# x1 of three supertiles in four turned by VectorE from blocks in device memory, and another order in the first two bodies

## What is computed

```python
xn = layer_norm(x) * gamma + beta
Q, K, V, gate = xn @ WQ.T + bQ, xn @ WK.T + bK, xn @ WV.T + bV, silu(xn @ Wg.T + bg)
for t: h = alpha * h + k_t v_t^T;  o_t = q_t h          # 16 heads, state 64 x 64
x1 = norm(x + x + (o * gate) @ WO.T + bO)               # no scale, no shift
gf = global_net(mean over the sequence of x1)           # 3 small layers
out = x1
for _ in range(3):                                      # coupling_net: 4 layers, GELU
    coupling = 0.1 + range * (0.7 * gf + 0.3 * coupling_net(out) - 0.5) * 2
    out = out + coupling * twist(out)
result = norm(x1 + out)
```

## Time and profile before

| | |
|---|---|
| median of 3 runs | 1736.63 us (1735.86 to 1736.78) |
| profiled execution, its own time | 1735.65 us |
| its span, first to last instruction | 1733.8 us |
| TensorE busy | 1670.2 us, 96% of the span |
| VectorE, ScalarE, POOL busy | 65%, 43%, 29% |
| mean granted TensorE clock | 0.990 |

### The profile page before, as it was taken

The page is one execution under the profiler, slowest core; times in us unless marked ns, Lnnn a source line. Parts: engine busy times, 40 slices in busy tenths (PEclk is TensorE's granted clock), DMA queues, the critical chain, the costliest instruction groups (busy, mean ns, idle before and its releaser), DMA issues.

```text
span 1733.8 us, 49923 instructions
## 1 busy us (share of the span) xinstructions
PE 1670.2 (96%) x21648; PEld 1329.6 (77%) x21648; DVE 1130.3 (65%) x2584; ACT 738.0 (43%) x1390; POOL 501.0 (29%) x496
## 2 busy tenths in 40 slices
PE   5999999999999999999999999999999999999992
PEld 4888888886688888888588888888768888888751
DVE  6667676765476767675566767676557676766654
ACT  3334343445443434245534343434544343434554
POOL 5323232331232323233032322323213232323301
PEclk9999999999999999999999999999999999999996
DMA  4000000001000000002000000000100000000101
GB/s 163 14 2 26 2 27 2 27 14 50 2 27 14 17 23 15 26 15 74 1 14 14 26 15 26 14 26 14 62 1 15 14 26 14 26 14 15 52 23 49
DMA packets 40249, 43.25 MB, mean 25 GB/s; under 512 B 4192, under 2 KB 38880, under 8 KB 40032
## 3 DMA queue, kind: packets, MB, share of 16 engines
q1 hardware_dynamic: 39888, 40.07, 7.1%
q10 hardware_dynamic: 144, 0.00, 0.0%
HBM read 23.29 MB, written 16.78 MB: 23 GB/s over the span
## 4 chain that ended last, share of the span: by engine, by line
PE 87%; ACT 4%; DVE 4%; issue 3%; POOL 1%; DMA 0%; ACTq 0%; SPq 0%; DVEq 0%; POOLq 0%
PE bank L1206 44%; PE bank L1286 11%; PE bank L1233 7%; PE bank L1273 6%; PE bank L1466 5%; PE bank L1250 4%; PE bank L1263 4%; PE bank L1242 3%; PE bank L1190 2%; PE bank L1488 1%; DVE att L959 1%; ACT q_sb L652 1%; ACT q_sb L734 1%; DVE q_sb L910 1%; ACT x_2b L751 1%
## 5 line engine op out<-in xcount | busy, mean ns | idle before, releaser
L520 POOL TENSOR_TENSOR k_end<-k_sc,pows 128x512 f32<-128x512 f32 x128 | 135.2, 1057 | 623.2 <-DVE k_sc L901 621.8
L652 ACT ACTIVATE q_sb<-q_sb,pows 128x384 f32<-128x384 f32 (+2 forms) x384 | 167.6, 499 | 243.6 <-DVE q_sb L910 243.6
L1075 DVE SCALAR_TENSOR_TENSOR h_seq<-h_seq,pows,bank 128x64 f32<-128x64 f32 x384 | 107.8, 281 | 240.5 <-PE bank L1250 229.8
L668 ACT ACTIVATE h_sc<-h_seq,pows 128x256 f32<-128x256 f32 x128 | 65.3, 510 | 418.8 <-DVE h_seq L1075 391.0
L529 POOL TENSOR_TENSOR o_lo<-o_g,o_hi 128x512 fp32r<-128x512 f32 x128 | 165.3, 1291 | 143.9 <-ACT o_hi L674 141.1
L959 DVE COPY_PREDICATED att<-causal,bank 128x1024 f32<-128x1024 int32 x128 | 169.0, 1320 | 0.5
L1286 PE MATMUL bank<-wo_hi,o_hi 128*128 128x256 f32 x512 | 147.9, 289 | 1.8 <-POOL o_lo L529 1.8
L674 ACT ACTIVATE o_hi<-o_g 128x512 fp32r<-128x512 f32 x128 | 80.8, 631 | 155.6 <-DVE o_g L975 155.6
L1286 PE MATMUL bank<-wo_hi,o_lo 128*128 128x256 f32 x512 | 143.1, 279 | 0.0
L1286 PE MATMUL bank<-wo_lo,o_hi 128*128 128x256 f32 x512 | 142.8, 279 | 0.0
L1273 PE MATMUL bank<-att,v_sb 128*64 128x128 f32 x2048 | 140.1, 279 | 0.6 <-DVE att L959 0.6
(11 more groups left out here) (214 smaller groups left out, 3883.4 us busy)
## 6 DMA issues: line engine op xcount, KB each, us to landing
x_in<-in_x SPq DMA_DIRECT2D x16, 512.0 KB, 3.9
x_rows<-x_nf SPq DMA_DIRECT2D x16, 512.0 KB, 2.9
x1t<-x_rows SPq DMA_DIRECT2D x32, 256.0 KB, 3.0
out_y<-x1t SPq DMA_DIRECT2D x32, 256.0 KB, 2.3
v_sb<-in_wq SPq DMA_DIRECT2D x1, 1024.0 KB, 6.2
v_sb<-in_wk SPq DMA_DIRECT2D x1, 1024.0 KB, 6.4
x1t<-in_wv SPq DMA_DIRECT2D x1, 1024.0 KB, 8.4
x1t<-in_wg SPq DMA_DIRECT2D x1, 1024.0 KB, 11.4
```

Source lines behind the costliest of these rows:

```text
L520: nc.gpsimd.tensor_tensor(k_end[:].rearrange("p (a z) (b r) -> p a (z b) r", z=2, r=BL), k_sc[:].rearrange("p (a z) (b r) -> p a (z b) r", ...
L652: last = nc.scalar.activation(q_sb[:, p % 2, d].rearrange("p (a z) n -> p a (z n)", z=2)[:, :, reach], q_sb[:, p % 2, 0].rearrange("p (a z ...
L1075: step = nc.vector.scalar_tensor_tensor(h_seq[:, c + 1, :] if c + 1 < NC else h_st[:, p, :], h_seq[:, c, :], pows[:, p, HP + 1:HP + 2], ba ...
```

## The change

x1 of s = 0 to 2 no longer goes through TensorE. `norm_apply` for it stands in the seam, in two pairs. SP stores the rows as before, waits for them to land and reads them back in four transfers (`blocks_brought`) into `x_f`: 32 rows and 32 columns make a block, each piece being 32 numbers (128 bytes), 1024 pieces in a transfer. In body 3 VectorE transposes 32x32 blocks from there into `x1t` (`x1_turned`, two instructions of 128x512). Waits that counted ScalarE's copies count `s_xv` where the first three supertiles are meant. In bodies 0 and 1 VectorE takes `queries_of` ahead of `masked`, and ScalarE `tokens_of` ahead of the gate. In body 5 `x_transposed` stands behind the transposes of `k_end`, and on ScalarE `x_scaled` behind `tokens_of`. TensorE's wait before the first output projection, in body 2, is for `s_r` and no longer for `s_x1c`.

```diff
@@ -78,6 +78,7 @@
         x_n = x_nf[:, 0, :].rearrange("p (c d) -> p c d", c=NC)
         x_f = x_nf[:, 1, :].rearrange("p (k n) -> p k n", k=KT)
+        x1_blocks = x_nf[:, 1, :].rearrange("p (k a n) -> p k a n", k=KT, n=BL)
         x_2b = sb("x_2b", [P, NC, D])
@@ -334,7 +337,9 @@
         x_rows = a["x"].rearrange("(i c p) d -> i p c d", c=NC, p=P)
         out_rows = out.rearrange("(i c p) d -> i p c d", c=NC, p=P)
-        x1_rows = nc.dram_tensor("x1_rows", (B * T, D), f32, kind="Internal").ap().rearrange("(i c p) d -> i p c d", c=NC, p=P)
+        x1_plain = nc.dram_tensor("x1_rows", (B * T, D), f32, kind="Internal").ap()
+        x1_rows = x1_plain.rearrange("(i c p) d -> i p c d", c=NC, p=P)
+        x1_in_blocks = x1_plain.rearrange("(i a t) (k q n) -> i q t k a n", a=ST // BL, t=BL, k=KT, q=P // BL)
@@ -372,6 +377,13 @@
                 sp.dma_start(x1_rows[step], x_n).then_inc(s_kept, 16)
+            def blocks_brought(step):
+
+                sp.wait_ge(s_xlo, step + 2 + C0)
+                sp.wait_ge(s_kept, (step + 1) * 16)
+                for q in range(P // BL):
+                    sp.dma_start(x1_blocks[q * BL:(q + 1) * BL], x1_in_blocks[step, q]).then_inc(s_xb, 16)
+
             def brought_back(b, t):
@@ -385,6 +397,7 @@
                     if s:
                         put_aside(it - 1)
+                        blocks_brought(it - 1)
                     if it + 1 < B * NS:
@@ -629,6 +646,8 @@
                 act.wait_ge(s_xt, step + 1)
                 act.wait_ge(s_xlo, step + C0)
+                if step > 1:
+                    act.wait_ge(s_xv, turned_by_vector((step - 1) // NS, (step - 1) % NS))
                 for k in range(KT):
@@ -673,11 +692,10 @@
                 nc.scalar.activation(o_hi[:, p % 2], o_g[:, p % 2], ACT.Copy).then_inc(s_ohi, 1)
-            def x1_copied(step, first_bank):
-
-                place = step % NS
-                act.wait_ge(s_x1t, step + 1 + C0)
-                act.wait_ge(s_out[place], step // NS * KT * 16 + C0)
+            def x1_copied(b, place, first_bank):
+
+                act.wait_ge(s_x1t, b + 1)
+                act.wait_ge(s_out[place], b * KT * 16 + C0)
                 for k in range(KT):
@@ -717,7 +735,7 @@
                     act.wait_ge(s_yp, (b + 1) * NS * NP - 1 + u + C0)
                 if u == NS * 2 - 2:
-                    act.wait_ge(s_x1c, (b + 1) * NS * KT + C0)
+                    act.wait_ge(s_x1c, (b + 1) * KT + C0)
                 nc.scalar.activation(halved(o_hi, u), x1_part(u), ACT.Copy).then_inc(s_xrh, 1)
@@ -784,15 +802,16 @@
                         if p + 1 < NP:
                             queries_shifted(p + 1, n + 1)
+                            if p < 2:
+                                tokens_of(n + 1)
                             act.wait_ge(s_og, n + C0)
                             gate_of(p + 1, n + 1)
+                            if p == NP - 2 and following:
+                                x_high(it + 1)
+                            if p > 1:
+                                tokens_of(n + 1)
                             if p == NP - 3 and following:
                                 x_scaled(it + 1)
-                            if p == NP - 2 and following:
-                                x_high(it + 1)
-                            tokens_of(n + 1)
-                            if p == 1 and s:
-                                x1_copied(it - 1, 6)
                             if p == 1 and b:
@@ -872,11 +891,12 @@
                 nc.vector.tensor_scalar(vare, mv[:, :, 1], EPS, None, ALU.add).then_inc(done, 1)
-            def norm_apply(dst, src, done):
-                for c in range(NC):
+            def norm_apply(dst, src, done, first=0, end=NC):
+                for c in range(first, end):
                     last = nc.vector.tensor_scalar(dst(c), src(c), mv[:, c, 0:1], rstd[:, c:c + 1],
                                                    ALU.subtract, ALU.mult)
-                last.then_inc(done, 1)
+                if end == NC:
+                    last.then_inc(done, 1)
@@ -885,11 +905,19 @@
                 dve.wait_ge(s_rstd, step + 1)
                 if step:
-                    dve.wait_ge(s_x1t, step - 1 + C0)
+                    dve.wait_ge(s_x1t, (step - 1) // NS)
                     dve.wait_ge(s_kept, (step - 1) * 16)
                 norm_apply(lambda c: x_n[:, c, :], lambda c: x_in[:, c, :], s_xn)
                 dve.wait_ge(s_xn, step + 1)
                 dve.sem_inc(s_xfree, 1)
+
+            def x1_turned(b, place):
+
+                dve.wait_ge(s_xb, (b * (NS - 1) + place + 1) * (P // BL) * 16)
+                dve.wait_ge(s_out[place], b * KT * 16 + C0)
+                for k in range(KT):
+                    nc.vector.transpose(x1t[:, k, place * ST:(place + 1) * ST],
+                                        x_f[:, k, :]).then_inc(s_xv, 1)
@@ -1085,17 +1113,19 @@
                         if p + 1 < NP:
                             keys_of(p + 1, n + 1)
-                            masked(n)
+                            if p > 1:
+                                masked(n)
                             if p == 0:
                                 dve.wait_ge(s_wolo, 1)
                             queries_of(p + 1, n + 1)
+                            if p < 2:
+                                masked(n)
                             if p == 2 and b:
                                 final_summed(b - 1, s)
                             if p == 5 and b:
                                 final_stats(b - 1, s)
-                            if p == 0 and s:
-                                dve.wait_ge(s_rs1, it)
-                                norm_apply(lambda c: x_n[:, c, :], lambda c: x_2b[:, c, :], s_x1)
+                            if p == NP - 5 and s:
+                                x1_turned(b, s - 1)
                             if p == NP - 5 and following:
@@ -1126,6 +1156,11 @@
                             if m == NC:
                                 norm_moments(s_r1)
+                            if m == NC + 2:
+                                dve.wait_ge(s_rs1, it + 1)
+                            if m > NC + 1:
+                                first = (m - NC - 2) * 2
+                                norm_apply(lambda c: x_n[:, c, :], lambda c: x_2b[:, c, :], s_x1, first, first + 2)
                     else:
@@ -1133,7 +1168,10 @@
                 for n, (first, end) in enumerate(((0, T - ST), (T - ST, T))):
-                    dve.wait_ge(s_x1c, (b * NS + NS - 1 + n) * KT + C0)
+                    if n:
+                        dve.wait_ge(s_x1c, (b + 1) * KT + C0)
+                    else:
+                        dve.wait_ge(s_xv, turned_by_vector(b, NS - 1))
                     nc.vector.tensor_reduce(msum[:, n, :], x1t[:, :, first:end], AX.X, ALU.add).then_inc(s_ms, 1)
@@ -1345,20 +1383,19 @@
                             pe.wait_ge(s_kev, n + 2 + C0)
                             project("g", p + 1, 0).then_inc(s_g, 1)
-                            if p == NP - 3 and following:
-                                pe.wait_ge(s_xn, it + 2)
-                                pe.wait_ge(s_att, n + 1 + C0)
-                                x_transposed()
                             if p == 2:
                                 pe.wait_ge(s_wolo, 1)
-                                pe.wait_ge(s_x1c, (it if s else b * NS) * KT + C0)
+                                if it:
+                                    pe.wait_ge(s_r, it * 2)
                             if p > 1:
                                 y_part(p - 2, n - 2)
                             pe.wait_ge(s_kend, n + 2 + C0)
                             pe.wait_ge(s_qev, n + 2 + C0)
                             keys_transposed().then_inc(s_kt, 1)
-                            if p == 1 and s:
-                                x1_transposed(it - 1, 6)
+                            if p == NP - 3 and following:
+                                pe.wait_ge(s_xn, it + 2)
+                                pe.wait_ge(s_att, n + 1 + C0)
+                                x_transposed()
                         else:
@@ -1414,7 +1451,7 @@
                     if t == 0 and c == 0:
                         pe.wait_ge(s_att, last_body + C0)
-                        pe.wait_ge(s_x1c, (b * NS + NS - 1) * KT + C0)
+                        pe.wait_ge(s_xv, turned_by_vector(b, NS - 1))
                     if t == 1 and c == 0:
```

12 lines of the change are left out of this document (8 added, 4 removed).

## The result

The changed kernel takes 1714.89 us (median of 4 runs, 1712.26 to 1715.32) against 1736.66 us for the kernel before (4 runs beside it, 1735.86 to 1736.78): a ratio of 0.9871, 95% interval 0.9857 to 0.9886. That is 21.8 us or 1.3% faster.

What follows compares the result with a forecast made beforehand. TensorE, busy 96%, was taken as the bound. Gains of 6.1, 1.5, 9.7 and 2.7 make 20.0 us, less 1.2 for the seam: 18.8 net, so 1716.85 profiled, 1717.8 us median; range 1713 to 1726 for 8 in 10.

Steps and rivals of the forecast that it cites:

- Point 1: Body 1 of 12 supertiles loses 16 x1 transposes on TensorE, 0.65 us each time.
- Point 2: Bodies 0 and 1: queries_of ahead of masked starts the k_end transposes 0.16 us earlier, leaving 0.3 margin for att.
- Point 3: Bodies 0 and 1: tokens_of ahead of the gate saves 0.22 us; in body 1 it keeps the hidden k_tok wait away.
- Point 4: Body 5: x_transposed moved behind the k_end transposes saves 0.18 us in 15 supertiles, with 0.5 margin before the scores.
- The seam: Moving x1's normalisation to the seam costs 0.1 us each time, 1.2 in all; bounds 0 to 5.
- The two transposes: Body 3: VectorE's pair of 128x512 transposes takes some 1.4 us, hidden in 1.99 idle with 0.6 left.
- The rival of slow transposes: Body 3: transposes at 1.25 us each overrun idle time by 0.5, 6 us in all, giving 1723.8; chance 0.09.
- The blocks: x1's 4096 pieces, 51 ns each, take 13 us plus 1.5, landing at 147, 12 us before body 3 wants them; no cost.
- The estimate of 1910: Kernel end if 4096 packets at 10.5 ns took 43 us, 16 more than there are; the prediction said the trace disagrees.
- the first rival: Late blocks stall VectorE, then TensorE, in body 3; gain eaten at 28.6 us, 1780 at 120 ns a piece; chance 0.07.

Runs made afterwards that it cites:

- the order alone: Kernel before with only the reorderings in bodies 0, 1 and 5, x1 still transposed on TensorE: 1720.82 us, ratio 0.9911.
- edit 2: VectorE taking queries_of ahead of masked in bodies 0 and 1; changed kernel with only this undone: 1720.43 us, ratio 0.9909.
- edit 3: ScalarE taking tokens_of ahead of the gate in bodies 0 and 1; changed kernel with only this undone: 1714.61 us, ratio 0.9875.
- the path of x1 alone: Changed kernel with the old order in bodies 0, 1 and 5, only the new x1 path kept: 1731.67 us, ratio 0.9974.
- the run with four: Changed kernel with four VectorE transposes instead of two in body 3: 1714.80 us, ratio 0.9877.
- where SP issues for 22.5 us: Changed kernel with twenty more transfers of 128-byte pieces issued by SP ahead of the four block transfers: 1715.22 us, ratio 0.9878.
- where it issues for 40.5: Changed kernel with forty more transfers of 128-byte pieces issued by SP ahead of the four block transfers: 1938.89 us, ratio 1.1167.

## Why the prediction was right, and where its steps were off

**What bounds the kernel.** Right. TensorE stayed the bound, and the time fell by what it no longer does or waits for.

**Point 1, the x1 transposes.** Right as a size (0.65 forecast, 0.64 between the order alone and the whole) and right that they hid a wait: taken away alone they give 0.37.

**Point 2, `queries_of` ahead of `masked`.** It was priced at 0.16. Body 0 is 0.47 shorter by edits 2 and 3 together, and 7.12 − 6.92 = 0.20 longer when edit 2 is undone. Its margin for `att`, 0.3, was measured as 0.27.

**Point 3, `tokens_of` ahead of the gate.** The step that failed is "this edit is what keeps it away". With ScalarE's old order the `k_tok` wait hardly returns: bodies 0 and 1 lose 0.07 and 0.01. Edit 2 makes `q_sb`, hence the shifted queries, hence the gate and `k_tok` all earlier. Edit 2 alone takes body 0 from 7.39 to 7.00, edit 3 alone to 7.12, and both to 6.92, so their gains of 0.39 and 0.27 don't add up to the 0.47. Both work on the same wait, and in full it stands only with both undone, 32 times in the run with the path of x1 alone. The forecast treated them as independent: it followed `k_tok` to what stands ahead of it on ScalarE and not further back, to what ScalarE itself waits for. For the time it made no difference, since both edits were in.

**The sizes of points 2 and 3** are the terms that were too small. Edit 3 takes the first 0.27 (7.39 to 7.12) where 0.22 stood in the sum, and edit 2 behind it 0.20 where 0.16 stood. 1.15 − 0.93 = 0.22 was a distance between starts of matmuls, read in a body whose updates begin in another way; the wait printed in the row of weight loads was 0.29, and weight loads without a wait follow after 0.82 and not 0.93. The sum counted the 0.22 in 20 bodies and the 0.16 in 32: 20 × 0.05 + 32 × 0.04 = 2.3 us, about the 2.1 by which bodies 0 and 1 beat the forecast.

**Point 4, `x_transposed` moved.** Right: 0.19 against 0.18, with the margin of 0.5 at the scores. Body 5 is 9.90 with the order alone and 10.10 with the path of x1 alone, so the gain is this edit's.

**The seam.** Priced at 0.1 each time, measured as 0.05 of gain with the norm there and the same without it: nothing. The second pair overlaps the wait for TensorE entirely. The lower bound would have been the right choice. With these terms the table's 22.8 is explained beside the 18.8 forecast: 2.1 in bodies 0 and 1, 1.8 in the seam and 0.1 in body 5. The medians show 21.8 and not 22.8; a spread of that size lies ahead of the first body and behind the last (last section).

**The two transposes.** 1.30 for 1.4, and hidden; 0.81 left where 0.6 was forecast. The rival of slow transposes was priced as if none of the delay were made good; the run with four showed that two thirds are.

**The blocks.** Right that they are free, far off in price: 13 ns a piece and 6.8 us from the first issue to the last landing, where 51 ns and 14.5 us were taken from pieces eight times as large. 1-KB pieces move 1024 / 51 = 20 bytes per ns of engine time and 128-byte pieces 128 / 13 = 10, so a small piece costs half the rate but not a fixed 51 ns. The Trainium skill (DMA: Bandwidth & Descriptors, Specifications) says that transfers under 512 bytes don't reach the full rate; the trace agrees, by that factor of two. Whether the engines read, modify and write there no run here shows. The estimate of 1910 took the 10.5 ns a packet that the Trainium skill (DMA: Bandwidth & Descriptors, Measured) gives for the floor of a transfer of 64 packets as a rate for any number of them. The trace disagrees with that use: 4096 pieces were moved within 6.0 us, 1.5 ns a piece over all sixteen engines. The edge that the first rival gave, 28.6 us from issue to use, isn't contradicted by either run: where SP issues for 22.5 us ahead of the last landing the cost is within the error, and where it issues for 40.5 the kernel is 12% slower.

## What to carry to other kernels

Where an engine is busy 96% of the time, compare the same pair of its instructions in two bodies, one with and one without a neighbour's delay: the small differences (0.16, 0.29), times the number of bodies, are the gain, and they are to be read on the row that shows the wait. Two edits that work on one wait are not two gains: follow the late operand back through all engines before giving the credit to the one that stands nearest. Rearrangement by small pieces through device memory cost TensorE and VectorE nothing here, with an idle queue and the use some 20 us away; when it does get late, the queue's next load gets late with it.
